# Ten of sixteen graphs get their broadcast rows by DMA, and GpSimd makes one attention's weights and one layer's quotients

## The reference

```python
x = _layernorm(x + _L0(x, adj, ...))   # 4-head dot-product attention, masked, then a projection
x = _layernorm(x + _L1(x, ...))        # one additive attention
x = _layernorm(x + _L2(x, adj, ...))   # additive attention with 8 heads
x = _layernorm(x + _L3(x, adj, ...))   # MLP, an unmasked additive attention ("l3"), MLP, a masked one ("l3b")

# layer 0, per head
scores = jnp.where(adj == 0, -inf, q @ k.T / sqrt(32)); attn = softmax(scores); out = attn @ v
# an additive attention: target i, source j
e = leaky_relu(s1[i] + s2[j], 0.2)
att = softmax(where(adj > 0, e, -big)) ; out = att @ h
```

## Time and profile before

| | us |
|---|---|
| median of 3 runs | 1079.1 |
| the profiled execution | 1080.22 |
| its span | 1078.4 |
| PE busy | 1024.1 (95% of the span) |
| DVE busy | 914.3 (85%) |
| ACT busy | 771.2 (72%) |
| POOL busy | 272.7 (25%) |
| `row<-line` DMAs | 128, of 256 KB, 3.7 us from issue to landing |

### The profile page before, as it was taken

The page is one execution under the profiler, slowest core; times in us unless marked ns, Lnnn a source line. Parts: engine busy times, 40 slices in busy tenths (PEclk is TensorE's granted clock), DMA queues, the critical chain, the costliest instruction groups (busy, mean ns, idle before and its releaser), DMA issues. The chain is left out here.

```text
span 1078.4 us, 26660 instructions
## 1 busy us (share of the span) xinstructions
PE 1024.1 (95%) x9189; PEld 760.1 (70%) x9189; DVE 914.3 (85%) x2533; ACT 771.2 (72%) x2029; POOL 272.7 (25%) x606
## 2 busy tenths in 40 slices
PE   7989999999999999999999999999999999899985
PEld 5667767667677777868577776777676777666784
DVE  4656999998999988999899799989899798988543
ACT  3979858775777788768886977868867875544543
POOL 1012414131323224222212332223213232220101
PEclk9999999999999999999999999999999999999998
DMA  4000212202020200202030031112020021020000
GB/s 127 2 11 12 90 29 63 70 21 76 16 78 14 90 11 21 80 22 79 2 100 11 12 90 56 35 33 69 21 80 2 25 67 60 30 72 19 11 11 20
DMA packets 30468, 46.81 MB, mean 43 GB/s; under 512 B 6912, under 2 KB 9216, under 8 KB 30336
## 3 DMA queue, kind: packets, MB, share of 16 engines
q1 hardware_dynamic: 29472, 44.84, 13.4%
q10 hardware_dynamic: 864, 0.26, 0.1%
HBM read 40.64 MB, written 4.46 MB: 42 GB/s over the span
## 5 line engine op out<-in xcount | busy, mean ns | idle before, releaser
L1230 DVE SCALAR_TENSOR_TENSOR P<-row,t2e,mask_t 128x512 f32<-128x512 f32 x512 | 355.9, 755 | 11.2 <-PE bank L608 10.4
L766 ACT ACTIVATE probs<-probs,neg_max 128x512 f32<-128x512 f32 x256 | 186.7, 732 | 35.6 <-DVE neg_max L1046 35.6
L1038 DVE CUSTOM_DVE_ANT_0 probs<-bank,mask_add 128x512 f32<-128x512 f32 x256 | 169.5, 677 | 20.4 <-PE bank L503 19.8
L776 ACT ACTIVATE probs_t<-bank 128x512 f32<-128x512 f32 x256 | 151.0, 610 | 12.7 <-PE bank L511 12.2
L511 PE MATMUL bank<-ident,probs 128*128 128x128 f32 x1024 | 142.7, 277 | 5.1 <-ACT probs L766 3.1
L511 PEld LDWEIGHTS bank<-ident,probs 128*128 128x128 f32 x1024 | 114.0, 141 | 37.5 <-ACT probs L766 19.9
L811 ACT ACTIVATE x<-x,shift_l,rstd_l 128x128 f32<-128x128 f32 x256 | 105.3, 487 | 38.9 <-POOL shift_l L1368 38.9
L608 PE MATMUL bank<-P,GH 128*32 128x512 f32 x1024 | 116.4, 595 | 4.5 <-issue 3.2
L653 PE MATMUL bank<-t,l_P 128*128 128x258 f32 x512 | 119.8, 383 | 1.0 <-DVE l_P L1152 0.9
L1353 POOL TENSOR_TENSOR rstd_l<-mv_l,ln_eps 128x4 f32<-128x4 f32 x64 | 16.1, 252 | 384.0 <-DVE mv_l L1092 383.8
L653 PEld LDWEIGHTS bank<-t,l_P 128*128 128x128 f32 x512 | 93.8, 190 | 16.7 <-issue 2.5
(11 more groups left out here) (168 smaller groups left out, 1922.5 us busy)
## 6 DMA issues: line engine op xcount, KB each, us to landing
row<-line SPq DMA_DIRECT2D x128, 256.0 KB, 3.7
x_in<-in_x SPq DMA_DIRECT2D x16, 256.0 KB, 2.8
out<-x SPq DMA_DIRECT2D x16, 256.0 KB, 2.0
l_P<-in_adj SPq DMA_DIRECT2D x4, 256.0 KB, 5.2
w_fc<-in_L_gnn_W_fc SPq DMA_DIRECT2D x1, 256.0 KB, 4.2
P<-in_L_gnn_a_fc SPq DMA_DIRECT2D x1, 256.0 KB, 3.5
line<-turned SPq DMA_DIRECT2D x16, 16.0 KB
w_cat<-in_L_gnn_W SPq DMA_DIRECT2D x2, 64.0 KB, 4.1
```

The lines of the kernel that those rows point to most:

```text
L766: act.activation(e, e, ACT.Exp, bias=neg_max[:, m:m + 1], scale=SCALE0, accum_out=g.of(den0)[:, m:m + 1])\
L776: act.activation(probs_t[c % 2][:, h, :, :].rearrange("p j n -> p (j n)"), ps("l0_t", g, m)[:, :], ACT.Copy)\
L1038: dve.tensor_tensor_reduce(probs[c % 2][:, h, :], ps("l0_s", g, m)[:, :], mask_add[:, c, :], 1.0, -3.0e38, ALU.add, ALU.max, row_max[:, m: ...
L1230: last = dve.scalar_tensor_tensor(P2[:, h % GROUP2, j, :], row(g, h)[:, :], g.of(t2e)[:, j, h:h + 1], mask_t[:, j, :], ALU.max, ALU.mult)
```

## The change

For graphs 2 to 11 (`ROWS_BY_DMA`), the row that `l0_rd`, `l1_s`, `l3_s` and `l3b_s` made on PE in a PSUM bank is made as in layer 2: DVE transposes a 128x32 tile (`turn`), SP writes it to DRAM (`lay_out`) and reads it back broadcast (`spread`, `l0_spread`), 256 KB each, into one of six `row` tiles in SBUF. From there POOL instead of DVE makes `l3_p` (4 instructions of 128x512) and `l0_o` (one), while DVE still makes `l1_p` and `l3b_p`, now from the SBUF tile. The other six graphs stay as they were.

For all graphs, q and its bias are scaled by -SCALE0, so that the scores are negated ("turned"): `l0_max` takes a minimum, which serves as the bias of `l0_exp` as it is, and `l0_neg` is gone. `l0_exp` now waits for its own head's `l0_max` instead of four.

All orders, the bank table and the table of row tiles are written anew.

```diff
-ROWS = 5
+ROWS = 6
+ROWS_BY_DMA = range(2, 12)
 ORDER = {
...
-        "g3e3k2f3k2f3g3a4f3f3b4g3l2c4d4t0m2o1f3f3u0f3p1p1f3e4g3q1Z0Z0Z0Z0r1Z0Z0Z0Z0Z0t0e4h3u0f4f4i3f4f4e4v0f4"
...
+        "a4t0g3f3f3u0f3f3b4q1j2c4g3k2e4k2r1d4e4f4f4f4t0f4e4u0f4l2f4f4f4v0g4e4w0i3f4f4f4f4g4f4g4a5x0b5y0y0c5d5"
...
+            def lay_out(n, turned):
+                def f(g, k):
+                    sp.wait_ge(*(sig if n == "l2" else dma_sig)(n + "_turned", g, 1))
+                    if n == "l0" and by_dma(g, 2):
+                        sp.wait_ge(*divided(g, back=2))
+                    sp.dma_start(g.of(line[n]).rearrange("r (q s) -> q r s", s=BLOCK),
+                                 turned[:, :]).then_inc(signal[n + "_rows"], 16)
+                return f
...
+            def spread(n):
+                def f(g, k):
+                    if k == 0:
+                        sp.wait_ge(*(sig if n == "l2" else dma_sig)(n + "_rows", g, 16))
+                    to, done = free_row(n + "_spread", g, k)
+                    sp.dma_start(to[:, :], g.of(line[n])[k * C:(k + 1) * C, :].rearrange("c p -> (c p)")
+                                 .rearrange("(o n) -> o n", o=1).broadcast_to([P, N_NODES])).then_inc(done, 16)
...
             def l0_y(g, k):
-                pe.wait_ge(*took("l0_rd", g))
+                pe.wait_ge(*divided(g))
...
             def l0_exp(g, m):
-                if m % HEADS0 == 0:
-                    act.wait_ge(*sig("neg_max0", g, m // HEADS0 + 1))
+                act.wait_ge(*took("l0_s", g, m))
...
-                act.activation(e, e, ACT.Exp, bias=neg_max[:, m:m + 1], scale=SCALE0, accum_out=g.of(den0)[:, m:m + 1])\
+                act.activation(e, e, ACT.Exp, bias=low0[:, m:m + 1], scale=-1.0, accum_out=g.of(den0)[:, m:m + 1])\
...
-            def l0_neg(g, c):
-                dve.wait_ge(*took("l0_s", g, HEADS0 * c + HEADS0 - 1))
-                if g.has(1):
-                    dve.wait_ge(*sig("exp0", g, HEADS0 * c + HEADS0, back=1))
-                q = slice(HEADS0 * c, HEADS0 * (c + 1))
-                dve.tensor_scalar(neg_max[:, q], row_max[:, q], -1.0e20, -SCALE0, ALU.max, ALU.mult)\
-                    .then_inc(signal["neg_max0"], 1)
...
+            def turn(n, column, made, turned):
...
+                    dve.transpose(turned[:, :], column(g)).then_inc(signal[n + "_turned"], 1)
...
+            def sources(n, g):
+                return row(n + "_spread", g)[:, :] if by_dma(g) else ps(n + "_s", g)[:, :]
...
-                    made = dve.scalar_tensor_tensor(q["P"][:, j, :], ps(n + "_s", g)[:, :], q["b"][:, j:j + 1],
+                    made = dve.scalar_tensor_tensor(q["P"][:, j, :], sources(n, g), q["b"][:, j:j + 1],
                                                     mask_t[:, j, :], ALU.max, ALU.mult)
...
+            def l0_o(g, k):
+                pool.wait_ge(*spread_done("l0_spread", g))
+                for c in range(C):
+                    pool.wait_ge(*took("l0_pv", g, c))
+                pool.wait_ge(*wrote("l0_y", g, back=1))
+                pool.tensor_tensor(o0_t[:, :], row("l0_spread", g)[:, :], o0_raw[:, :], ALU.mult).then_inc(signal["o0_made"], 1)
+
+            def l3_p(g, j):
+                q = gat["l3"]
+                if j == 0:
+                    pool.wait_ge(*sig("l3_b", g, 3))
+                    pool.wait_ge(*spread_done("l3_spread", g))
+                    pool.wait_ge(*wrote("l3_o", g, C - 1, back=1))
+                made = pool.tensor_scalar(q["P"][:, j, :], row("l3_spread", g)[:, :], q["g"][:, j:j + 1], q["b"][:, j:j + 1],
+                                          ALU.mult, ALU.max)
```

More of the change, by code:

```diff
@@ L17 @@
 SCALE0 = float(DH0) ** -0.5
-MASKED = -1.0e30
+MASKED, LOWEST = 1.0e30, 1.0e20
 LN_EPS = 1e-5
@@ L205, in bank_uses, with row_uses @@
     return used
+def row_uses():
+    used, transfers, last, at = {}, [0] * ROWS, [None] * ROWS, 0
+    for name, g, k in turns("sp"):
+        if name.endswith("_spread"):
+            r = int(ROW_OF_USE[at])
+            at += 1
+            transfers[r] += 1
+            used[name, k, g.i] = r, transfers[r], last[r]
+            last[r] = name, k, g
+    return used
 def build_program(nc, x, adj, w, out):
     use = bank_uses()
+    row_use = row_uses()
     with ExitStack() as ctx:
@@ L320, in build_program @@
         for n in GATS:
-            for what, k in (("c4", 1), ("dd", 2), ("b", 3)):
+            for what, k in (("c4", 1), ("dd", 2), ("b", 3), ("turned", 1), ("p", 1)):
                 sem(f"{n}_{what}", k)
@@ L359, in empty, with by_dma, dma_sig, sources_read @@
             return bank[b]
-        def row(g, h):
-            return rows[(HEADS2 * g.i + h) % ROWS]
-        def row_done(g, h):
-            n = HEADS2 * g.i + h
-            return row_filled[n % ROWS], 16 * (n // ROWS + 1)
-        line2 = [nc.dram_tensor(f"line2_{q}", [HEADS2 * C, P], F32, kind="Internal").ap() for q in range(2)]
+        def by_dma(g, back=0):
+            return g.i - back in ROWS_BY_DMA
+        def dma_sig(name, g, k=1, back=0):
+            return signal[name], per_graph[name] * ROWS_BY_DMA.index(g.i - back) + k
+        def sources_read(n, g, back=0):
+            return dma_sig(n + "_p", g, 1, back) if by_dma(g, back) else took(n + "_s", g, 0, back)
+        def divided(g, back=0):
+            return dma_sig("o0_made", g, 1, back) if by_dma(g, back) else took("l0_rd", g, 0, back)
+        def row(stage, g, k=0):
+            return rows[row_use[stage, k, g.i][0]]
+        def spread_done(stage, g, k=0):
+            r, transfers, _ = row_use[stage, k, g.i]
+            return row_filled[r], 16 * transfers
+        def row_read(stage, g, k):
+            if stage == "l2_spread":
+                return sig("p2_made", g, k + 1)
+            return divided(g) if stage == "l0_spread" else sources_read(stage[:-len("_spread")], g)
+        line = {n: [nc.dram_tensor(f"{n}_line{q}", [BLOCK, P], F32, kind="Internal").ap() for q in range(2)]
+                for n in ("l0", "l1", "l2", "l3", "l3b")}
         x_v = x.rearrange("b (p c) d -> b p c d", c=C)
@@ new lines, in free_row @@
+            def free_row(stage, g, k):
+                r, _, last = row_use[stage, k, g.i]
+                if last:
+                    sp.wait_ge(*row_read(last[0], last[2], last[1]))
+                return rows[r], row_filled[r]
+            def spread(n):
[5 more added lines that the diff above has]
+                                 .rearrange("(o n) -> o n", o=1).broadcast_to([P, N_NODES])).then_inc(done, 16)
+                return f
@@ L781, in l0_ov @@
                 if g.has(1):
-                    act.wait_ge(*took("l0_rd", g, back=1))
+                    act.wait_ge(*divided(g, back=1))
                 act.activation(o0_raw[:, c * P:(c + 1) * P], ps("l0_pv", g, c)[:, 0:P], ACT.Copy)\
@@ L1210, in l2_cap @@
                     .then_inc(signal["small2_made"], 1)
[L1212 to L1217 removed]
             def l2_p(g, h):
[L1220 removed]
+                dve.wait_ge(*spread_done("l2_spread", g, h))
                 if h == 0:
@@ L1326, in _ @@
             pool.memset(ln_eps[:, :], LN_EPS)
+            for t in [rden0] + [gat[n]["R"] for n in GATS]:
+                pool.memset(t[:, :], 0.0)
             for t in GH:
```

341 lines of the change are left out of this document (180 added, 161 removed), and 11 rows, old and new, of the table STAGES.

## The result

The changed kernel takes 1105.7 us (median of 6 runs, 1099.3 to 1111.1) against 1078.8 for the kernel before beside it (6 runs): ratio 1.0255, 95% interval 1.0232 to 1.0278, 27 us slower. The forecast was 1051 with a range of 1038 to 1070. The profiled execution took 1106.58, its span is 1104.5.

The account below looks back on a forecast made before the run. PE, 98% busy in the middle, was taken as the bound. From 1080.2 us, 29.1 of PE work and 2.0 of `warm` came off, 3 of latency came on: 1052.1, given as 1051; range 1038 to 1070.

Parts of the forecast that it names:

- What bounds the kernel now: Middle 783 us: PE is 98% busy, so work taken off PE shortens the time if nothing arrives later.
- PE's terms: Removed `l0_rd` -10.6 us, spreads of l1, l3 and l3b -18.5, `warm` -2.0: -31.1 us on PE.
- POOL's price: New POOL work: `l3_p` 0.9 us each, `l0_o` 1.14, together 47 us more, POOL then at about 320 us.
- The prediction's own sign of being wrong: Forecast is wrong if POOL's 128x512 instructions take over 2 us, or DVE's share of the middle passes PE's.
- the slower rival: At the l3 weights, PE reaches `l3_o` before POOL has ended its four `l3_p`: 1085 us, chance 0.09.
- I charge 3 us in all: Latency: late rows, SP's queue, and normalisation steps behind `l3_p` on POOL cost 3 us, ends 0 and 20.
- The detour: Rows through DRAM arrive about 6.2 us after their column, PE took 0.6; as a rival, 1066 us, chance 0.22.
- under 10 us: Expected sign in the changed profile: DVE or POOL waits under 10 us for `row<-line`.
- the good case: PE's waits for POOL's `o_t` or `l_P` sum to a few us; 30 or more mean the slower case.
- The negated scores: In layer 0, `l0_neg` goes from DVE; ACT's shorter wait before `l0_exp` can only help, counted as nothing.
- DVE's term: On DVE, the removed `l0_neg`: 64 instructions, 11.3 us.
- The contention: POOL's new instructions hold up DVE's SBUF reads by 12 us, ends 0 and 45; L1230 rises about 10 us.

Follow-up runs that it names:

- e14: Kernel before with 50 more `warm` stages on PE where the spreads stand: 1095.7 us, ratio 1.0180.
- e10: Kernel before with negated scores, old orders; graphs 2 to 11 leave out `l0_rd`, `l1_s`, `l3_s`, `l3b_s`, DVE reads a constant tile: 1076.6 us, ratio 0.9990.
- e11: e10 with DVE's `l3_p` of graphs 2 to 11 also cut to 128x4: 1075.0 us, ratio 0.9971.
- e5: Changed kernel with each of POOL's 40 `l3_p` made a product of 128x4: 1087.9 us, ratio 1.0092.
- e2: Changed kernel with `l3_p` of the ten graphs on DVE instead of POOL, from the same SBUF row: 1104.3 us, ratio 1.0256.
- e6: e5 with POOL's ten `l0_o` made products of 128x4 too: 1082.1 us, ratio 1.0049.
- e3: Kernel before with only the negated scores, `l0_neg` gone: 1077.6 us, ratio 1.0004.
- e1: Changed kernel with each `l3_p` on POOL making 128 of its 512 columns: 1088.2 us, ratio 1.0108.
- e8: Kernel before, orders kept, with 40 `TENSOR_SCALAR` and 10 `TENSOR_TENSOR` of 128x512 added on POOL, results unread: 1137.5 us, ratio 1.0559.
- e7: e6 with the 40 added broadcasts filling 16 partitions instead of 128: 1082.1 us, ratio 1.0043.
- e9: e6 without the added writes and broadcasts; readers take a constant tile once DVE's transposition is there: 1081.7 us, ratio 1.0043.
- e13: e11 with the power of each normalisation on POOL replaced by a product of constants: 1064.6 us, ratio 0.9876.
- e4: Changed kernel with `l3_p` on POOL as one operation instead of two, the maximum left out: 1098.1 us, ratio 1.0200.

## Why the prediction was wrong

**The step that failed first** is the one in "What bounds the kernel now": "work taken off PE there comes off the time if nothing arrives later than it does now". The 98% were read rightly, and e14 shows that PE's stream is full. But five streams in a fixed order wait for one another's results. Take PE's work away and PE arrives early and waits: e10 has 17 us more idle time in the middle, and the time of before (ratio 0.9990). The condition had to be "if everything arrives earlier than it does now". The statement that PE hardly waits was no evidence of slack in the others. On DVE it looks alike: 40 `l3_p` removed from the old orders give 1.6 us (e10 to e11), added to the new ones they cost 16 to 18 (e5 to e2). The forecast had its whole gain, 29 to 31 us, from this step, and e10 gives 1. e10 is a bound for the old orders only; whether orders exist that turn the removed work into time was not tested beyond the ones of the change.

**PE's terms were too large besides.** I took busy over count of each group. e10 removed those groups and PE's busy time fell by 20.6 us, not 29.1; the 50 stages of e14 have 30.0 us busy as a group (75.7 against 45.7 in the earlier trace rows) and added 17.2. A group's busy time still overlaps with the matmuls of other groups at its ends, and stages of four short matmuls are nearly all ends. In the changed kernel the fall is 10.1 us, less again, and the granted clock accounts for that: busy time times the mean clock is 1018 us before (1024.1 x 0.994), 1000 after (1014.0 x 0.986) and 1000 in e10 (1003.5 x 0.996). This is an estimate, since the mean is over the span, but by it the same work is gone in both, and some 8 us came back because PE ran longer at its lower level. The forecast had taken full clock for granted. The low stretches follow waits of PE, so they are first a consequence of the loss; how much of the 27 us goes through the clock no run shows. The warning that a mean over-counts stopped one step short.

**POOL's price.** `l3_p` was put at 0.9 us between 0.20 and 1.14. It is 2.06 us undisturbed and 2.47 on average, beyond the upper bound, which came from two-input products and was wrongly taken to cover a form that no row showed. The prediction's own sign of being wrong, over 2 us, came true. `l0_o` at 1.14 was near (1.26 undisturbed). POOL's time rose by 150 us where I had 47: 112 for the new instructions, and 38 more for the old ones (`rstd`, L1431 after, has a mean of 370 ns, before of 252), of which 36 are there in e6 too. That DVE's new reads from SBUF hold them up has a sign in e10: there DVE reads a tile in SBUF in place of PSUM in the old orders, POOL's own work is unchanged, and POOL is busy 292.0 us instead of 273.9 in e3. That is half of the 36; the rest is not taken apart. I had named the point from which the slower rival decides, 1.5 us per `l3_p`, and a chance of 0.09: the form was unmeasured, and that alone should have carried more. By e1 and e5 the length of `l3_p` is worth 17.5 us, `l0_o` another 5.

**"On POOL, `var`, `pow` and `shift` stand behind `l3_p` pieces ... I charge 3 us in all."** The mechanism was named and mis-sized. ACT's wait for `shift` rose from 38.9 to 80.6 us; 64 of it are there without POOL's new work (e6), so that work adds 16. e8 shows that such a load by itself costs 60 us in the old orders. The new ones take it better: all of POOL's new work costs them 23 us.

**The detour** was right as far as it was tested: the row is late by about 6 us and nothing comes of it once POOL's new work is cut (e7, e9). One sign was missed: POOL waits 67.4 us for the row of `l0_o` in the changed kernel, where I had "under 10 us" for `row<-line`, and what stands behind it on POOL waits too. In e6 that wait is 38.4 us, and taking the detour out (e9) gave nothing. PE's waits for `l_P` and `o_t` on POOL are 8.2 and 4.5 us in the matmuls' view, "a few us" as I had for the good case. **The negated scores** were right at nothing beyond DVE's term, which itself was worth nothing (e3). The contention is 6 us on L1300 (362.1 against 355.9 us busy), where I had 10. But the 80 `l1_p` and `l3b_p` from SBUF cost 778 ns each, where I had 695: 6.6 us more, so the 12 us charged to contention were about right together. `l0_neg` gave 7 us of its 11.3 (e3). DVE is at 895, not 880; the rest of that gap was not taken apart.

**The account**, from 1078: the new orders without the PE work and with POOL's new work nearly gone, +5 (e6, e9); `l0_o` on POOL, +5; `l3_p` on POOL, +17.5. That makes some 1106. Each term is what one removal gave in this sequence; in another sequence they can come out otherwise, as e13 shows for the old orders. Why the new orders with less work on PE and DVE stand 5 us above the old ones with the same work left out (e9 against e10) I didn't test; ACT's wait for `shift` (65.9 against 47.5 us) and DVE's wait for PE at `l2_p` (31.6 against 11.0) are longer there. None of the kernels run that compute the whole result is faster than the one before; e3 is the same.

The rival that came true is the slower one, 1085 foreseen, on a base that never had the gain. Its mechanism, PE waiting for the weights at `l3_o`, is there: 8.2 us of waits, 0.4 in e4, where the time is 7.6 us shorter. Beside it stand the normalisations queued behind `l3_p`: `shift` is waited for 80.6, 70.3, 67.4 and 63.8 us in after, e4, e1 and e5. The runs shorten both at once, so how the 17.5 us divide between them is not shown.

## What to carry to other kernels

A share of 98% says that work added to this engine costs its price, not that work removed gives it back; in a kernel of hand-ordered streams ask of each removal what makes the other streams earlier. Before building a detour, run its upper bound: leave the work out, put a constant in its place, keep the orders (e10). Here it would have said, before anything was built, that the old orders have nothing to gain from it, and that all of the gain had to come from new ones. And an engine that is 25% busy is no free place when short instructions on the path of every layer stand in its queue: price the longest new instruction ahead of them, and measure a form that no row shows.

## What the runs showed of the hardware

- POOL's `TENSOR_SCALAR` with two per-partition scalars: the shortest takes 2.06 us for 128x512 (mean 2.47), 0.78 for 128x128 (mean 1.20, e1), and 1.56 with one operation at 128x512 (mean 1.83, e4). From the two widths, as an estimate, 0.35 us don't shrink with the width. It is slower than a `TENSOR_TENSOR` with two tensor inputs of the same size (1.26 undisturbed; 1.04 in e8, where both inputs are one tile). The same `TENSOR_SCALAR` on DVE takes 0.55 us from SBUF (e2), 0.80 from PSUM.
- A tiny instruction of DVE can last as long as a two-input one of POOL beside it. After, first POOL, then DVE; `l_dd` (L1196) has a median of 226 ns in 32, and this is its longest. That POOL held it up is inferred from the two ends, 317.60 and 317.63:

```profile
316.32 1.28 POOL L1482 TENSOR_TENSOR o_t<-row,o_raw 128x512 f32<-128x512 f32 x1 [21.53 <-DMA row<-l_line]
```

```profile
316.50 1.13 DVE L1196 TENSOR_SCALAR l_dd<-t,l_ndmax 128x4 f32<-128x4 f32 x1
```

The Trainium skill, page "GPSIMD Engine Reference", section "8. Key points", names contention with VectorE instructions in a 2-port perf mode or with two SBUF inputs. This one has a single tensor input in SBUF, so by that sentence only the first case would be left, and no row here shows the mode. Its section "4.1 Engine selection" advised against the move. The kernel became slower, though `l3_p` on DVE was no better in these orders (e2). The prices there are about two times VectorE's for two inputs, which the trace bears out (1.26 us against 0.68), and roughly line rate for one input, which it does not: the one-input form was the slow one, 2.06 us against 0.55 on DVE.
